# One layer of adaLN attention and feed-forward on Trainium2: later waits on GpSimd, the query weights' low part on GpSimd, other orders of VectorE and ScalarE in batch 0

## The reference

```
mod = silu(c) @ wmod -> sa, ca, ga, sb, cb, gb        # per batch; ga, gb kept away from zero
h   = layernorm(x) * (1 + ca) + sa
Xn  = layernorm(h) * gamma + beta
Q, K, V = split(Xn @ W_in + b_in); K, V = rotary(K), rotary(V)
A   = 0.5 * sum over rows(K/|K| * V/|V|) + 0.5        # one vector of 512 per batch
x   = x + ga * ((A * Q) @ W_out + b_out + h)
h   = layernorm(x) * (1 + cb) + sb
x   = x + gb * (relu(h @ W_up.T) @ W_down.T + (sum of top-2 softmax weights) * (h @ W_expert))
```

## Time and profile before

| what | value |
|---|---|
| median of 3 runs | 401.78 us (401.06 to 402.11) |
| time of the profiled execution | 400.71 us |
| its span, first to last instruction | 398.9 us |
| TensorE busy | 371.0 us (93%), mean granted clock 0.966 of full |
| VectorE, ScalarE, GpSimd busy | 260.5, 167.3, 110.4 us |

### The profile page before, as it was taken

How to read it: one execution, slowest core, us unless ns; L and a number is a source line. 1 busy time by engine, 2 the same in 40 slices (tenths; PEclk the granted TensorE clock), 3 DMA queues, 4 the chain that set the end, 5 groups by cost and what they waited for, 6 DMA issues and landing times.

```text
span 398.9 us, 4661 instructions
## 1 busy us (share of the span) xinstructions
PE 371.0 (93%) x1664; PEld 288.7 (72%) x1664; DVE 260.5 (65%) x520; ACT 167.3 (42%) x293; POOL 110.4 (28%) x108
## 2 busy tenths in 40 slices
PE   4997979295999899999999999998999999999996
PEld 0146858284787687888888878886788878887885
DVE  0768899567797868988597665683751556084354
ACT  1237354765533781137602774217313711361120
POOL 0115063266283252932353240640001000100000
PEclk9987999688899999999999999999999999999999
DMA  7987961004001100000000001100200020011002
GB/s 226 403 328 246 359 268 55 0 0 151 9 2 45 35 0 2 22 6 0 2 0 28 0 0 54 53 28 0 79 28 0 27 81 0 0 55 53 2 0 105
DMA packets 10950, 27.42 MB, mean 69 GB/s; under 512 B 1184, under 2 KB 1568, under 8 KB 9776
## 3 DMA queue, kind: packets, MB, share of 16 engines
q1 hardware_dynamic: 10928, 27.13, 19.1%
HBM read 22.90 MB, written 4.23 MB: 68 GB/s over the span
## 4 chain that ended last, share of the span: by engine, by line
PE 73%; DVE 7%; issue 5%; DMA 5%; ACT 4%; POOL 3%; SPq 2%; POOLq 0%; DVEq 0%; ACTq 0%
PE ps L1035 21%; PE ps L1036 21%; PE ps L1037 21%; PE ps L1059 3%; PE ps L1042 3%; DMA gate_bc<-mod_rows 3%; DMA xs<-in_wmod 2%; DVE w_lo L615 1%; ACT sqj L444 1%; PE ps L1050 1%; PE ps L1162 1%; PE ps L1163 1%; POOL xs L349 1%; POOL hb L347 1%; DVE hb L659 1%
## 5 line engine op out<-in xcount | busy, mean ns | idle before, releaser
L1035 PE MATMUL ps<-w_hi,t_hi 128*128 128x512 f32 x192 | 76.0, 396 | 2.3 <-DVE prod L704 2.2
L1036 PE MATMUL ps<-w_lo,t_hi 128*128 128x512 f32 x192 | 75.2, 392 | 0.0
L1037 PE MATMUL ps<-w_hi,t_lo 128*128 128x512 f32 x192 | 75.2, 392 | 0.0
L1035 PE MATMUL ps<-w_hi,g_hi 128*128 128x512 f32 (+1 forms) x132 | 52.4, 397 | 4.2 <-DVE g_lo L745 4.2
L1035 PE MATMUL ps<-t_hi,w_hi 128*128 128x512 f32 x128 | 51.8, 405 | 0.0
L1036 PE MATMUL ps<-w_lo,g_hi 128*128 128x512 f32 (+1 forms) x132 | 51.5, 390 | 0.0
L1037 PE MATMUL ps<-w_hi,g_lo 128*128 128x512 f32 (+1 forms) x132 | 51.5, 390 | 0.0
L1036 PE MATMUL ps<-t_lo,w_hi 128*128 128x512 f32 x128 | 50.6, 395 | 0.0
L1037 PE MATMUL ps<-t_hi,w_lo 128*128 128x512 f32 x128 | 50.4, 394 | 0.0
L685 DVE TENSOR_TENSOR t_lo<-ps,t_hi 128x512 fp32r<-128x512 f32 x32 | 21.9, 687 | 37.2 <-ACT t_hi L495 37.1
L1035 PEld LDWEIGHTS ps<-w_hi,t_hi 128*128 128x128 f32 x192 | 36.5, 190 | 10.9 <-issue 3.4
(11 more groups left out here) (130 smaller groups left out, 616.6 us busy)
## 6 DMA issues: line engine op xcount, KB each, us to landing
xs<-in_X SPq DMA_DIRECT2D x4, 1024.0 KB, 7.8
stage<-in_w SPq DMA_DIRECT2D x4, 1024.0 KB, 6.0
out<-xs SPq DMA_DIRECT2D x15, 256.0 KB, 2.0
xs<-in_wmod SPq DMA_DIRECT2D x3, 1024.0 KB, 10.1
xs<-in_wmod SPq DMA_DIRECT2D x8, 256.0 KB, 6.5
stage<-in_w SPq DMA_DIRECT2D x8, 256.0 KB, 9.6
gate_bc<-mod_rows SPq DMA_DIRECT2D x8, 256.0 KB, 6.7
gate_bc<-in_wmod SPq DMA_DIRECT2D x1, 1024.0 KB, 12.7
```

What stands on the lines that cost most here:

```text
L1035: mm(dst, l_hi, r_hi, start=start, stop=False)
L1036: mm(dst, l_hi, r_lo, start=False, stop=False)
L1037: return mm(dst, l_lo, r_hi, start=False, stop=stop)
```

## The change

- **GpSimd.** The three waits ahead of batch 0 go to where they are needed: `gate_out` (the modulation's rows have left `hb`) to just ahead of `scale_rows(1, 0)`, `const_in` ahead of `base(0, t)`, `ga_in` ahead of the first `x2_out` in `attention(1)`. Ahead of `base(0, t)` a new wait stands, for the four O low parts of VectorE (`wlo_out`).
- **Q low part.** VectorE's 128x2048 `split_lo(2)` goes; GpSimd makes it as four 128x512 pieces after the K low part (`low_part(2, ..)`, semaphore `wlo_q`). TensorE's first Q chunk and SP's `load_x(2)` wait for that.
- **VectorE, batch 0.** `x_stats(1)` and `x_aggr(1)` now stand ahead of the waits for the constants and the modulation rows. `h_row`, `h_stats`, `h_aggr` of tiles 2 and 3 and `x_mean(2)` now stand ahead of `kv_products(0, 2)`, `h_shift(1, 2, 2)` behind it (before: ahead of `kv_products(0, 3)`).
- **ScalarE, batch 0.** `split_hi(3)` moves from behind the `t_evac` of batch 1 to between `norm_sums(0, 1)` and `x_sums(2)`.

```
@@ SP @@
             sp.wait_ge(wlo_k, NC)
             sp.dma_start(w_raw[3], w[3]).then_inc(w_in[3], 16)
-            sp.wait_ge(wlo, 1)
+            sp.wait_ge(wlo_q, NC)
             load_x(2)
...
-            sp.wait_ge(wlo, 2)
+            sp.wait_ge(wlo, 1)
             sp.dma_start(w_raw[6], w[6]).then_inc(w_in[6], 16)
@@ GpSimd @@
                 weight(b, 0)
                 if b == 0:
+                    pool.wait_ge(gate_out, 32)
                     scale_rows(1, 0)
...
                         scale_rows(b + 1, 1)
+                    if b == 1:
+                        pool.wait_ge(ga_in, B * 16)
                     x2_out(b - 1, 2)
...
                 pool.wait_ge(afold, b * 3 + 3)
                 if b == 0:
+                    pool.wait_ge(const_in, N_CONST)
+                    pool.wait_ge(wlo_out, NC)
                     for t in range(NT):
                         base(0, t)
...
             low_part(0, whi_k, (1, 2, 3, 4), wlo_k)
-            pool.wait_ge(gate_out, 32)
-            pool.wait_ge(const_in, N_CONST)
-            pool.wait_ge(ga_in, B * 16)
+            low_part(2, whi, (1,) * NC, wlo_q)
@@ ScalarE @@
                 norm_sums(b, 1)
                 if b == 0:
+                    split_hi(3)
                     x_sums(2)
...
                     t_evac(b + 1, c)
-                if b == 0:
-                    split_hi(3)
@@ VectorE @@
                     x_stats(1)
                     x_aggr(1)
+                    dve.wait_ge(const_in, N_CONST)
+                    dve.wait_ge(row_out, 32)
                 kv_rows(b, 0)
...
                     h_shift(1, 0, 2)
-                kv_products(b, 2)
-                if 0 < b < B - 1:
-                    h_shift(b + 1, 2, 2)
-                elif b == 0:
                     h_row(1, 2)
                     h_row(1, 3)
                     h_stats(1, 2)
                     h_stats(1, 3)
                     h_aggr(1, 2, 2)
                     x_mean(2)
+                kv_products(b, 2)
+                if b < B - 1:
+                    h_shift(b + 1, 2, 2)
...
                 kv_rows(b, 3)
-                if b == 0:
-                    h_shift(1, 2, 2)
                 kv_products(b, 3)
...
-            split_lo(2)
-            dve.wait_ge(const_in, N_CONST)
-            dve.wait_ge(row_out, 32)
@@ TensorE @@
-                    if c == 0:
-                        pe.wait_ge(wlo, 1)
+                    if b == 0 and c == 0:
+                        pe.wait_ge(wlo_q, NC)
```

More of the change, by code:

```diff
@@ L151, in build @@
         wlo = sem("wlo")
+        wlo_q = sem("wlo_q")
         wlo_k, wlo_v = sem("wlo_k"), sem("wlo_v")
@@ L606, in split_lo @@
             def split_lo(i):
-                dve.wait_ge(whi, {2: 1, 4: 4}[i])
+                dve.wait_ge(whi, 4)
                 r = W_ORDER[i]
@@ L822, in attention @@
                     h_shift(1, 0, 2)
[L823 to L826, removed]
                     h_row(1, 2)
@@ L1168, in ffn @@
                     out_rows_of(B - 1)
-                pe.wait_ge(wlo, 2)
+                pe.wait_ge(wlo, 1)
                 for c in range(NC):
```

## The result

| | before | after |
|---|---|---|
| first comparison, median (executions) | 401.94 us (4) | 388.50 us (4), 388.38 to 389.97 |
| ratio, 95% interval | | 0.9669, 0.9629 to 0.9709 |
| second comparison (run `after_again`) | 401.33 us (17) | 389.66 us (6), ratio 0.9702, 0.9671 to 0.9732 |
| third comparison (run `after_third`) | 401.53 us (11) | 390.55 us (6), ratio 0.9740, 0.9701 to 0.9780 |
| span of the profiled execution, granted clock | 398.9 us, 0.966 | 386.6 us, 0.985 |

What follows compares the result with a forecast made beforehand. TensorE, busy for 93% of the span, could gain only from its waits and half-clock stretches. 5.35 + 5.1 - 0.65 = 9.8 us, so 401.78 - 9.8 = 392.0 us, range 389.0 to 396.2.

Steps and rivals of the forecast that it cites:

- The first half and the second half (5.35): Batch 0: both `kprod` waits go and VectorE's chain runs earlier, so TensorE gets `z` 5.35 us sooner, at 71.75.
- direct-shift rival: Batch 0: `kv_sum(0, 0)` stays in the shadow of `scale_rows` and moves by only 1.0; gain 8.1, 393.7 us; chance 0.08.
- The output product (5.1): First output tile: the 4.2 us `g_lo` wait and its clock fall go, the tile ends at 92.5 instead of 102.97.
- its slow matmuls behind the gap then stay as they are: Behind TensorE's wait for `z`: the clock still falls in the 4.05 us gap, leaving the slow matmuls there unchanged.
- The rival in which the clock holds: TensorE's 4.05 us gap before `z`: the clock does not fall, 2.7 to 2.8 us more gain, 389.2 us; chance 0.12.
- The rival in which the clock falls in the first output tile: First output tile, TensorE busy 0.68 of every 1.27 us: TensorE only 7.45 us ahead, 394.3 us; chance 0.10.
- What batch 1 gives back (0.65): Batch 1: the chain feeding `transposes(2, 0)` gains 9.8, TensorE 10.45, so TensorE waits some 0.65 us longer there.
- late-`base` rival: Batch 1: GpSimd's `base` pieces take 1.77 us and last until 98.7, `o_evac(0, 3)` comes at 104.4; 395.0 us; chance 0.13.
- all engines are shifted alike: From the wait before `transposes(2, 0)` on: nothing is changed and every engine moves by the same amount.
- The slower rival: GpSimd's Q low part ahead of `rstd_x(1)` makes GpSimd late; whole gain eaten only from 4.1 us a piece; chance 0.04.
- the prediction's rule (four times the excess over 1.66): GpSimd's Q pieces: nothing is lost up to 1.66 us a piece, beyond it four times the excess.

Runs made afterwards that it cites:

- after_again: The changed kernel, unchanged, measured again beside the kernel before; 389.66 us, ratio 0.9702.
- after_third: The changed kernel, unchanged, once more beside the kernel before; 390.55 us, ratio 0.9740.
- undo_waits: Changed kernel with GpSimd's three waits put back ahead of batch 0, behind the Q low part; 395.67 us.
- only_waits: Kernel before with only GpSimd's three waits moved as in the change; 397.28 us.
- undo_dve_order: Changed kernel with VectorE's order in batch 0 put back, `kv_products(0, 2)` ahead of `h_row(1, 2)` and `x_mean(2)`; 392.11 us.
- undo_q_low: Changed kernel with the Q weights' low part back on VectorE, ahead of `x_stats(1)`; 391.09 us.
- undo_o_hi: Changed kernel with ScalarE's `split_hi(3)` back behind the `t_evac` of batch 1; 390.78 us.
- undo_base_wait: Changed kernel without GpSimd's wait for the O weights' low part ahead of `base(0, t)`; 393.54 us.
- warm_gap: Changed kernel with 16 unused filler matmuls of 128x512 on TensorE in its wait for `z`; 387.89 us.
- before_again: The kernel before, unchanged, measured and profiled again; 401.23 us.
- pool_pieces: Changed kernel with three more GpSimd subtractions of 128x512 behind the Q low part; 394.79 us.

## Why the prediction was right and where it was wrong

The range missed the first comparison by 0.5 us; the gain was 9.8 by the forecast, 13.4 in that comparison and 11.0 to 11.7 in the repeats. Step by step, from the bodies, in the prediction's own sum 5.35 + 5.1 - 0.65:

**The first half and the second half (5.35): right, 5.6.** GpSimd's pieces took 1.26 us each, the x rows landed when taken, `rstd_x(1)` ended at 47.0, both `kprod` waits went. From the first transposes, `kv_sum(0, 0)` began 21.1 us in, forecast 50.75 - 29.70 = 21.05. That is 3.8 us sooner than before: 2.1 from `x_shift(1)`, 1.6 from the two products that no longer run beside `scale_rows`. `undo_waits` and `only_waits` show the waits alone to be worth 3.8 to 3.9 of z, `undo_dve_order` VectorE's order 2.1 (they overlap in part, together it is 5.6), `undo_q_low` the Q part nothing, `undo_o_hi` ScalarE's move nothing in z. The wait for `z` is 4.16 us, forecast 4.05. The direct-shift rival falls: 3.9 us of z hang on waits that hold `rstd_x(1)` back by 2.2.

**The output product (5.1): mis-sized, 6.6.** This is the step that failed. The last matmul of the first output tile, in before and then in after:

```profile
102.38 0.58 PE L1037 MATMUL ps<-w_hi,g_lo 128*128 128x512 f32 x1
```

```profile
89.07 0.40 PE L1036 MATMUL ps<-w_hi,g_lo 128*128 128x512 f32 x1
```

From `transposes(1, 0)` to the end of that tile it was 102.97 - 77.10 = 25.9 us, and is 89.47 - 70.25 = 19.2 (20.1 in `after_again`); forecast 92.5 - 71.75 = 20.75. Two terms were carried over from before that do not hold. First, `ab_col`: the prediction left it its 1.03 us, because `base` starts just then. It took 0.16; VectorE issued it 0.13 us ahead of `base`. In the four profiles in which `base` was already running (both of before, `undo_base_wait`, `only_waits`) it took 1.03. So the first `g_lo` is there before TensorE is free, and the tile takes 3.8 us and not 4.5: 0.7 us, the same in `after_again`. Second, the matmuls behind the gap: "its slow matmuls behind the gap then stay as they are". In this profile they don't, and from `transposes(1, 0)` to the end of `kv_tile(1, 0)` it is 15.4 us instead of 16.24: 0.8 us. Windows of the kernel after; the columns are those of the earlier trace rows:

```profile
66.00:70.00 4.00, 0.09 (x1) 0.00 (x0) 3.68 (x9) 3.68 (x10) 1.06 (x2) 1.00 0.00 0
71.00:72.00 1.00, 1.00 (x6) 0.90 (x4) 0.00 (x0) 0.97 (x2) 0.00 (x0) 0.53 0.00 0
73.00:74.00 1.00, 1.00 (x4) 0.79 (x3) 0.42 (x2) 0.60 (x1) 0.00 (x0) 0.50 0.00 0
74.00:75.00 1.00, 1.00 (x5) 0.82 (x4) 1.00 (x2) 0.00 (x0) 0.00 (x0) 0.77 0.00 0
```

TensorE stands still from 66.1 to 70.25, and the clock falls only when it works again, and is back before 75. The eight transposes took 1.25 us against 1.97. In `after_again` the clock fell while TensorE still stood still, they took 1.97, and the forecast's 16.24 was met (16.3):

```profile
70.00:71.00 1.00, 0.00 (x0) 0.00 (x0) 1.00 (x5) 1.00 (x3) 0.47 (x1) 0.70 0.00 0
```

In `after_third` they took 1.32. So in one program the gap of 3.6 to 4.2 us costs up to 0.9 us more in one profile than in another, and why it falls one way or the other the record doesn't show. The rival in which the clock holds was half right, and the 2.8 us it asked for bound this from above; `warm_gap` measured 1.4 to 2.3.

The kernel before has a spread here too: in `before_again` the four O pieces took 6.92 us, in the first profile 5.79, and the wait for `g_lo` was 5.3 us instead of 4.2. The prediction's "about 7 us" for them is a median times four and not what its own trace had (88.35 to 94.1); its sum goes by the ends and doesn't use it.

The rival in which the clock falls in the first output tile did not come: the waits there are 0.20 and 0.31 us, and the granted clock stays at 1.00.

**What batch 1 gives back (0.65): 1.2, at another place.** `base` ran 10.11 us, not 11.8, since the O pieces no longer lie beside it, and from the first transposes `o_evac(0, 3)` came 1.7 us sooner than forecast. The late-`base` rival falls. But TensorE, further ahead than forecast, meets `kprod(1, 1)`:

```profile
109.83 0.47 PE L1034 MATMUL ps<-w_hi,t_hi 128*128 128x512 f32 x1 [1.31 <-DVE prod L707]
121.76 1.09 PE L1058 MATMUL ps<-idn,z 128*128 128x128 f32 x8 [0.79 <-ACT z L485]
```

The wait before `transposes(2, 0)` is 0.79 as in the earlier trace rows, not 1.4; the longer one was put in the wrong tile. From there to the end both kernels take 264.8 to 264.9 us, as "all engines are shifted alike" has it. The sum is 5.6 + 6.6 - 1.2 = 11.0, 1.2 us more than forecast.

**Outside the sum.** The other 2.4 of the 13.4 us are no part of the change's mechanism: 1.26 us between the two profiles in the front, and 1.1 because the profiled execution of before was 1.2 under its median (401.94) while that of after was 0.1 under its own. Both are luck of the executions drawn: the forecast had no term for the clock of the front, and its range no share for it, though the time of one program differs by 4.9 us. Pooled (16 executions of after, the 58 of before), the medians are 389.95 and 401.3, 11.4 apart, and 389.95 lies inside the range.

**The slower rival.** It did not come, GpSimd's pieces being cheap. Its slope was wrong. The prediction let GpSimd lose nothing until `weight(0, 0)` is held. `pool_pieces` held `rstd_x(1)` by 2.8 us, 1.2 of them free for `weight(0, 0)`, and z lost 4.4: `x_shift(1)` falls back among `scale_rows`, and that costs before the weight does. By this one point, pieces of about 2 us each (1.26 and a quarter of 2.8, an estimate) would cost z some 4.4 us, where the prediction's rule (four times the excess over 1.66) gives 1.2; no run shows at which price the whole gain is gone.

## What to carry to other kernels

A wait that several steps of an in-order queue don't need is worth more than its own length when what it delays falls into the time of another engine's long instructions: 2.2 us of delay of a 128x4 instruction were worth 3.9 us at the end of the chain. Before sizing the work behind a gap, don't take the durations of the trace as they are: those that ran beside another engine, or at half clock, have to be priced at both values, and both ends kept in the range. Give the total of a kernel like this one a share of clock noise as well (here 387.7 to 392.9 us for one program), and compare profiles from an event behind the noise.

## What the hardware showed that was not expected

- The granted clock of TensorE differs between executions of one program: the same eight matmuls in the front took 3.60 us in some profiles and 4.96 to 5.65 in the others, and executions as a whole differed by up to 4.9 us. Ahead of them stand 32 matmul records of 128x4.
- Filling a 4 us wait of TensorE with 16 matmuls whose results nobody uses made the kernel 1.4 to 2.4 us faster (body against body, and median against median).
- A GpSimd subtraction of 128x512 took 1.26 us with two inputs, and 1.01 us with one tensor as both inputs.
- A VectorE instruction on 128x4 numbers (`ab_col`) took 1.03 us in the four profiles where GpSimd's 128x512 additions were already running, and 0.16 us where it was issued 0.13 us ahead of the first of them. The price isn't fixed: another of 128x4 (`x_shift(2)`), beside the same additions, took 0.15 us in one profile of before and 1.27 in the other.
